# Attention scores split in two half-array parts in two planes, with single row maxima of one head beside score parts of another

## The reference, cut to what matters

```
q = src @ q_w ; k = src @ k_w ; v = src @ v_w        # 16 heads of 16
q = q scaled per head by a sigmoid-like gate of (q, scale_w), and by 16 ** -0.5
out = softmax(q @ k.T) @ v                           # per batch of 2048 tokens and head
```

## Time and profile before

| what | value |
|---|---|
| median of 3 runs | 2716.38 us (2714.47 to 2716.59) |
| the profiled execution | 2711.36 us |
| its span | 2709.6 us |
| mean granted clock of TensorE | 0.954 of full |
| busy PE / DVE / ACT / POOL | 93% / 80% / 64% / 32% of the span |

### The profile page before, as it was taken

The page is one execution under the profiler, slowest core; times in us unless marked ns, Lnnn a source line. Parts: engine busy times, 40 slices in busy tenths (PEclk is TensorE's granted clock), DMA queues, the critical chain, the costliest instruction groups (busy, mean ns, idle before and its releaser), DMA issues. The chain is left out here.

```text
span 2709.6 us, 40900 instructions
## 1 busy us (share of the span) xinstructions
PE 2507.0 (93%) x14248; PEld 1049.3 (39%) x14248; DVE 2172.1 (80%) x4357; ACT 1746.9 (64%) x2263; POOL 858.2 (32%) x991
## 2 busy tenths in 40 slices
PE   6799999999468999999999999999999999886995
PEld 6366666666341222222222222222222222464563
DVE  4577777787737889999899999898999995493885
ACT  2678877777130777777777777777777778322663
POOL 1377777777740111101110110111100000244563
PEclk9899999999785999999999999999999999886998
DMA  2322232222340030303004021030030000225884
GB/s 87 97 83 75 83 99 85 80 81 87 99 116 17 13 59 13 59 13 59 13 1 60 13 40 21 13 59 1 13 60 1 2 1 1 77 70 187 286 289 143
DMA packets 111524, 179.91 MB, mean 66 GB/s; under 512 B 18824, under 2 KB 85792, under 8 KB 106056
## 3 DMA queue, kind: packets, MB, share of 16 engines
q1 hardware_dynamic: 102984, 159.16, 22.0%
q0 software_dynamic: 6016, 15.41, 1.5%
q10 hardware_dynamic: 2320, 2.74, 0.3%
HBM read 150.42 MB, written 31.21 MB: 67 GB/s over the span
## 5 line engine op out<-in xcount | busy, mean ns | idle before, releaser
L1415 DVE TENSOR_REDUCE max_part<-round_psum 128x1 f32<-128x512 f32 x2048 | 1312.6, 685 | 107.3 <-PE round_psum L1344 93.5
L1387 ACT ACTIVATE p_exp<-score_psum 128x1024 f32<-128x1024 f32 x1024 | 992.5, 1022 | 282.7 <-PE score_psum L1332 282.5
L1364 PE MATMUL pv_psum<-p_exp,values 128*17 128x512 f32 x4096 | 539.7, 598 | 0.0
L1332 PE MATMUL score_psum<-q_stack,k_stack 99*128 99x512 bf16 (+1 forms) x2048 | 537.6, 383 | 1.5 <-DMA q_stack<-max_rows 0.7
L1344 PE MATMUL round_psum<-k_stack,q_stack 64*128 64x512 bf16 x2048 | 434.6, 395 | 15.4 <-DMA k_stack<-qk_rows 12.6
L1344 PEld LDWEIGHTS round_psum<-k_stack,q_stack 64*128 64x128 bf16 x2048 | 104.4, 93 | 687.0 <-DVE max_part L1415 565.2
L559 PE MATMUL rot<-tokens_t,w_in 128*128 128x512 f32 x576 | 274.5, 605 | 15.7 <-DVE bc_conv L697 12.7
L1332 PEld LDWEIGHTS score_psum<-q_stack,k_stack 99*128 99x128 bf16 (+1 forms) x2048 | 162.2, 98 | 259.4 <-ACT p_exp L1387 98.6
L1448 POOL CAST max_parts<-max_neg 128x16 bf16<-128x16 f32 x96 | 20.2, 211 | 655.3 <-DVE max_neg L1421 626.4
L766 POOL TENSOR_TENSOR decay<-cum_rows_in,scan_cum 128x1024 f32<-128x1024 f32 x64 | 121.4, 1897 | 109.0 <-PE y_psum L588 57.3
L941 POOL TENSOR_SCALAR q_scale<-q_scale 128x512 f32<-128x512 f32 x16 | 9.9, 618 | 434.3 <-ACT q_scale L923 434.3
(11 more groups left out here) (247 smaller groups left out, 3293.5 us busy)
## 6 DMA issues: line engine op xcount, KB each, us to landing
expert_w<-in_expert_w SPq DMA_DIRECT2D x39, 1028.0 KB, 5.7
cum_rows_in<-cum_rows SPq DMA_DIRECT2D x64, 512.0 KB, 3.8
cum_pairs_in<-cum_rows SPq DMA_DIRECT2D x120, 128.0 KB, 3.7
qk_rows<-qk_parts SPq DMA_DIRECT2D x64, 192.0 KB, 3.1
q_stack<-qk_rows SPq DMA_DIRECT2D x84, 128.0 KB, 7.7
k_stack<-qk_rows SPq DMA_DIRECT2D x84, 128.0 KB, 8.7
token_rows<-tokens SPq DMA_DIRECT2D x16, 512.0 KB, 3.4
x_in<-in_x SPq DMA_DIRECT2D x8, 512.0 KB, 8.5
```

The lines of the kernel that those rows point to most:

```text
L1332: m = nc.tensor.matmul(ebank[i][:, odd, :], ks[rows, n % 2, h, k * P:(k + 1) * P], qs[rows, n % 2, h, q * BLK:(q + 1) * BLK], start=True, ...
L1364: m = nc.tensor.matmul(pv[h * 32:h * 32 + VW, :], V[:, b * KT + k, g * HG + h, :], pt[:, (k * 2 + h // 2) % 4, h % 2, :], start=(k == 0), ...
L1387: nc.scalar.activation(pt[:, (k * 2 + i) % 4, :, :], ebank[i][:, :, :], ACT.Exp).then_inc(*exped.up(u, k, i))
L1415: nc.vector.tensor_reduce(mx[:, c * HG + h, keys:keys + 1], bank[step][:, :], AX_X, ALU.max).then_inc(*maxed.up(u, k, i))
```

## The change

Each head's rest rows (35) now lie in the same half of the array as its main rows, in a second plane of the stacks: head h has its main rows in plane `h // 2 * 2` and its rest rows in the plane after it. Heads 0 and 1 share these two planes, one in each half, as do heads 2 and 3. The number of rows moved by DMA into the stacks is the same; the zeros between are no longer needed.

A score is now two matmuls into the same bank that accumulate: `main` (64 rows, starts the sum) and `rest` (35 rows, ends it). In a step the twelve half-array matmuls stand in six pairs of neighbours, one in either half: maximum 0 and main 1; main 0 and rest 1; rest 0 and maximum 1; maximum 2 and main 3; main 2 and rest 3; rest 2 and maximum 3. Weighing and the due work follow. Main 1 and main 3 wait for ACT's reading of their tile a step ago; rest 0 and rest 2 release ACT; rest 1 of a unit's first step waits for the DMAs of the maximum rows.

```
-REST_AT = [slice(MAIN, MAIN + REST + MROWS), slice(0, REST + MROWS)]
+REST_AT = [slice(at.start, at.start + REST + MROWS) for at in MAIN_AT]
 MROWS_AT = [slice(at.stop - MROWS, at.stop) for at in REST_AT]
-ALL_AT = [slice(0, REST_AT[0].stop), slice(0, P)]
-GAP = slice(REST_AT[1].stop, MAIN)
+def main_of(h):
+    return MAIN_AT[h % 2], h // 2 * 2
+def rest_of(h):
+    return REST_AT[h % 2], h // 2 * 2 + 1
...
-            nc.sync.dma_start(dst[term_rows(t, odd), slot, odd::2, cols],
+            nc.sync.dma_start(dst[term_rows(t, odd), slot, t // 4::2, cols],
                               rows[odd]).then_inc(*S.stacked[slot].up(n, j, t, kind, odd))
...
                     for slot in range(2):
-                        for kind, tile, at, odd, rows in (("ones", S.ks, MROWS_AT[0], 0, gap[0:MROWS, :]),
-                                                          ("both", S.ks, slice(MROWS_AT[1].start, MAIN), 1, gap),
-                                                          ("gap", S.qs, GAP, 1, gap[MROWS:, :])):
-                            nc.sync.dma_start(tile[at, slot, odd::2, :].bitcast(F32),
-                                              over_mid(rows, HG // 2)).then_inc(*S.filled.up(slot, kind))
+                        for odd in range(2):
+                            nc.sync.dma_start(S.ks[MROWS_AT[odd], slot, 1::2, :].bitcast(F32),
+                                              over_mid(io["ones_rows"], HG // 2)).then_inc(*S.filled.up(slot, odd))
...
-        if scoring:
-            yield "score", u, k, 0
-            yield "score", u, k, 1
-        if ahead:
-            yield "max", mu, mk, 0
-            yield "max", mu, mk, 1
+        for left, right in ((("max", 0), ("main", 1)),
+                            (("main", 0), ("rest", 1)),
+                            (("rest", 0), ("max", 1)),
+                            (("max", 2), ("main", 3)),
+                            (("main", 2), ("rest", 3)),
+                            (("rest", 2), ("max", 3))):
+            for what, i in (left, right):
+                if what == "max" and ahead:
+                    yield what, mu, mk, i
+                if what != "max" and scoring:
+                    yield what, u, k, i
         if weighing:
             yield "weigh", *divmod(t - 1, KT), 0
-        if ahead:
-            yield "max", mu, mk, 2
-            yield "max", mu, mk, 3
         yield from due.get(t, [])
...
-                        nc.sync.dma_start(qs[MROWS_AT[h % 2], n % 2, h, q * BLK:(q + 1) * BLK],
+                        nc.sync.dma_start(qs[MROWS_AT[h % 2], n % 2, rest_of(h)[1], q * BLK:(q + 1) * BLK],
...
-                if what == "score":
+                if what == "main":
                     n, q = UNITS[u]
-                    if k == 0 and i == 0:
+                    rows, plane = main_of(i)
+                    if i % 2 and (u, k) != (0, 0):
+                        pe.wait_ge(*exped.at(*back(u, k, 1), i // 2))
+                    nc.tensor.matmul(ebank[i // 2][:, i % 2, :], ks[rows, n % 2, plane, k * P:(k + 1) * P],
+                                     qs[rows, n % 2, plane, q * BLK:(q + 1) * BLK], start=True, stop=False)
+                if what == "rest":
+                    n, q = UNITS[u]
+                    rows, plane = rest_of(i)
+                    if k == 0 and i == 1:
                         pe.wait_ge(*max_row[u % 2].at(u, HG - 1))
                         if u == 0:
                             pe.wait_ge(*S.filled.all())
-                    if (u, k) != (0, 0):
-                        pe.wait_ge(*exped.at(*back(u, k, 1), i))
-                    for odd in range(2):
-                        h, rows = i * 2 + odd, ALL_AT[odd]
-                        m = nc.tensor.matmul(ebank[i][:, odd, :], ks[rows, n % 2, h, k * P:(k + 1) * P],
-                                             qs[rows, n % 2, h, q * BLK:(q + 1) * BLK], start=True, stop=True)
-                    m.then_inc(*scored.up(u, k, i))
+                    m = nc.tensor.matmul(ebank[i // 2][:, i % 2, :], ks[rows, n % 2, plane, k * P:(k + 1) * P],
+                                         qs[rows, n % 2, plane, q * BLK:(q + 1) * BLK], start=False, stop=True)
+                    if i % 2 == 0:
+                        m.then_inc(*scored.up(u, k, i // 2))
```

More of the change, by code:

```diff
@@ L864, in __init__ @@
         self.loaded = sems.dma("w_qk_load", range(2))
-        self.filled = sems.dma("rows_fill", [(slot, what) for slot in range(2) for what in ("ones", "both", "gap")])
+        self.filled = sems.dma("rows_fill", [(slot, odd) for slot in range(2) for odd in range(2)])
         self.projected = sems.events("qk_projected", blocks)
@@ L1057, in _ @@
                 if (what, b) == ("load", NBLK - 1):
-                    gap = io["gap_rows"]
                     for slot in range(2):
-                        for kind, tile, at, odd, rows in (("ones", S.ks, MROWS_AT[0], 0, gap[0:MROWS, :]),
-                                                          ("both", S.ks, slice(MROWS_AT[1].start, MAIN), 1, gap),
-                                                          ("gap", S.qs, GAP, 1, gap[MROWS:, :])):
-                            nc.sync.dma_start(tile[at, slot, odd::2, :].bitcast(F32),
-                                              over_mid(rows, HG // 2)).then_inc(*S.filled.up(slot, kind))
+                        for odd in range(2):
+                            nc.sync.dma_start(S.ks[MROWS_AT[odd], slot, 1::2, :].bitcast(F32),
+                                              over_mid(io["ones_rows"], HG // 2)).then_inc(*S.filled.up(slot, odd))
                 if what == "residual":
@@ L1342, in _ @@
                         pe.wait_ge(*bank_read(before[step]))
-                    rows = MAIN_AT[h % 2]
-                    nc.tensor.matmul(bank[step][:, :], qs[rows, n % 2, h, at:at + P],
-                                     ks[rows, n % 2, h, keys * BLK:(keys + 1) * BLK], start=True,
+                    rows, plane = main_of(h)
+                    nc.tensor.matmul(bank[step][:, :], qs[rows, n % 2, plane, at:at + P],
+                                     ks[rows, n % 2, plane, keys * BLK:(keys + 1) * BLK], start=True,
                                      stop=True).then_inc(*summed.up(u, k, i))
@@ L1382, in _ @@
                 what, u, k, i = step
-                if what == "score":
-                    act.wait_ge(*scored.at(u, k, i))
+                if what == "rest" and i % 2 == 0:
+                    pair = i // 2
+                    act.wait_ge(*scored.at(u, k, pair))
                     if (u, k) >= (0, 2):
-                        act.wait_ge(*weighed.at(*back(u, k, 2), i))
-                    nc.scalar.activation(pt[:, (k * 2 + i) % 4, :, :], ebank[i][:, :, :],
-                                         ACT.Exp).then_inc(*exped.up(u, k, i))
+                        act.wait_ge(*weighed.at(*back(u, k, 2), pair))
+                    nc.scalar.activation(pt[:, (k * 2 + pair) % 4, :, :], ebank[pair][:, :, :],
+                                         ACT.Exp).then_inc(*exped.up(u, k, pair))
                 if what == "turn_rows":
@@ L2244, in layout @@
     o["v_w"] = kt(a["v_w"])
-    gap = np.zeros((MAIN - REST, SEQ // 2), np.uint32)
-    gap[0:MROWS] = 0x3F803F80
-    o["gap_rows"] = gap.view(np.float32)
+    o["ones_rows"] = np.full((MROWS, SEQ // 2), 0x3F803F80, np.uint32).view(np.float32)
     q = a["q_w"].reshape(KD, P, NG, HG * HD)
```

## The result

The changed kernel takes 2655.17 us (median of 4, 2651.04 to 2657.95), the kernel before 2716.49 (4 runs): a ratio of 0.9773, with a 95% interval of 0.9756 to 0.979. That is 61 us less; 52 were forecast. The profiled execution has a span of 2649.2 us, 60.4 less than before; 58.4 of that lie between the first and the last weighing of attention.

What follows compares the result with a forecast made beforehand. PE was taken to set the 2.60 us step, with DVE close behind. Terms -64 + 9 - 6 - 3 + 12 = -52 us gave 2716.4 - 52 = 2664; own range 2645 to 2690 (0.67), wider range 2630 to 2710.

Steps and rivals of the forecast that it cites:

- The step: A plain attention step falls from 2.60 to 2.47 us: -64 us over 492 steps with maxima.
- the first unknown: Whether a half's next load and matmul follow without a gap: 0 to 0.05 us per slot, taken as 0.
- (b): Weight loads show at the five slot boundaries: at 0.05 us each, a step of 2.65, kernel 2753; chance 0.09.
- (c): The full weight load shows, 0.10 us for each: a step of 2.90, kernel 2876; chance 0.02.
- The ring: Three banks rotate over four maxima per step; maximum 3 needs maximum 0's bank, so PE waits 0.07 us.
- Rival (a): Maximum 3's bank is already free by 1.10 us: a step of 2.40, -98 instead of -64, kernel 2630; chance 0.17.
- Rival (d): No change: DVE cannot start reduces closer than 0.65 us while PE writes the other banks; chance 0.05.
- Turned rows: Steps with turned rows keep the work and about 0.12 us of wait at maximum 2: 31 x 0.11 = -3 us.
- Negation: The negation delays maximum 3 by some 0.2 us, as now a maximum: nothing.
- Casts: In 28 steps with two casts ACT is late and main 3 stalls 0.3 us: +9 us.
- Turned output: DVE reduces maximum 0 only after the output's five operations: 1.08 us against 0.69 before, 31 x 0.39 = +12 us.
- Projections and scale matmuls: Now placed after weighing, they lose a bank wait: 0.14 x 42 = -6 us.

Runs made afterwards that it cites:

- the shortened reduce: Changed kernel with DVE's reduce of maximum 0 cut from 512 to 448 columns: 2626.65 us, ratio 0.9676.
- the run beside the moved output: The changed kernel itself, run on the same chip as a version with the turned output put between maximum 3 and weighing: 2652.16 us (that version 2648.55).

## Why the prediction was right, point by point

**The step.** 2.48 was seen where 2.47 was forecast. The slots follow each other 0.22 apart, so no load shows: the first unknown was taken right, and rivals (b) and (c) are out. Of the evidence for them, the three maxima of the earlier trace rows told the truth, and the 0.05 of the f32 scale matmul did not carry over. The ring costs what the chain of the earlier trace rows said: maximum 3 starts 1.18 after maximum 0 (forecast 1.17), and the shortened reduce shows that this link is the bound. Rival (a) is out. Rival (d) is too: DVE's reduces are 0.62 apart in a plain step, and 0.61 where DVE catches up behind a negation (its row further down). The other signs named are there as well: DVE is busy for all of the 7 us from 2200, neither main 1 nor main 3 waits in a plain step, and a step with turned output takes 3.56. One sign was too narrow: the load of maximum 2 waits for a bank too, at no cost. Between the medians, 2.604 and 2.474, lie 0.13 us a step, and 492 x 0.13 is 64 us, as forecast.

**The inserts** sum to about +5 us, where +12 was forecast. That is 7 of the 9 us by which the forecast fell short; the other 2 lie ahead of the first weighing. One of the five terms was right, the turned output. The other four, one of them put at nothing, were off by 4 to 9 us each, and partly cancel: that their sum came so near is luck. The prediction also missed what three of them share. It found that maximum 3 waits 0.07 us for its bank in every step, but not that another delay of PE in the same step runs inside this wait, and costs only what exceeds it. Rows of the changed kernel, first DVE around a negation, then PE at the weighings of the same stretch and at the turned rows:

```profile
2044.59 0.22 DVE L1435 TENSOR_REDUCE max_neg<-max_part 128x16 f32<-128x64 f32 x1
2044.92 4.96 DVE L1429 TENSOR_REDUCE max_part<-round_psum 128x1 f32<-128x512 f32 x8
```

```profile
2043.14 1.05 PE L1377 MATMUL pv_psum<-p_exp,values 128*17 128x512 f32 x8
...
2045.98 1.05 PE L1377 MATMUL pv_psum<-p_exp,values 128*17 128x512 f32 x8
...
2048.45 1.05 PE L1377 MATMUL pv_psum<-p_exp,values 128*17 128x512 f32 x8
2049.32 0.39 PE L1365 MATMUL round_psum<-const_ident_bf,max_parts 128*12 128x128 bf16 x4
2051.13 1.05 PE L1377 MATMUL pv_psum<-p_exp,values 128*17 128x512 f32 x8
```

- Turned rows: 2048.45 to 2051.13 is 2.68, so they cost 0.20 where 0.55 was paid before; 0.44 was forecast. The transposes start 0.87 after weighing, while a maximum starts 0.98 after it, and the wait of maximum 2 for its bank (0.07) runs inside that of maximum 3. That is -9 us instead of -3, for in four more cases, where a projection stands in the same step, nothing is gained.
- Negation: 2043.14 to 2045.98 is 2.84, a cost of 0.37. The prediction had some 0.2 for it before (the trace has 0.21) and put the difference at nothing. DVE has little slack (its eight reduces after it start (4.96 - 0.68)/7 = 0.61 apart), so the 0.33 from the negation to the reduce of the next maximum goes to the ring whole. Over the steps with a negation that is +4 us.
- Casts, forecast at +9. The timeline of PE and ACT in such a step:

```profile
1490.68 1.14 ACT L937 CAST qk_parts<-qk_raw 128x512 bf16<-128x512 f32 x2
1491.71 4.04 ACT L1401 ACTIVATE p_exp<-score_psum 128x1024 f32<-128x1024 f32 x4
```

```profile
1491.96 1.05 PE L1377 MATMUL pv_psum<-p_exp,values 128*17 128x512 f32 x8
...
1493.40 0.59 PE L1357 MATMUL round_psum<-k_stack,q_stack 64*128 64x512 bf16 x2
1493.71 0.49 PE L1335 MATMUL score_psum<-q_stack,k_stack 64*128 64x512 bf16 x2
...
1494.47 1.05 PE L1377 MATMUL pv_psum<-p_exp,values 128*17 128x512 f32 x8
```

ACT goes on to the exponentials 1.03 after it began the casts, not 1.2, for its operations overlap in the trace. Main 3 starts 0.31 after the line before, 0.09 late, where 0.3 was forecast; the ring had 0.07 of waiting to give, and the step takes 2.51 instead of 2.475. The place of the stall was right, but not its size or what it costs: some 0.03 us in about half of the 28 steps, under 1 us in all.

- Turned output, forecast 1.08, being its source:

```profile
2061.03 1.05 PE L1377 MATMUL pv_psum<-p_exp,values 128*17 128x512 f32 x8
2062.02 0.66 PE L1386 MATMUL round_psum<-const_f,pv_out 128*128 128x128 f32 x4
...
2062.71 0.26 DVE L1444 RECIPROCAL rden<-round_psum 128x16 f32<-128x16 f32 x1 [0.26 <-PE round_psum L1386]
...
2063.54 3.75 DVE L1429 TENSOR_REDUCE max_part<-round_psum 128x1 f32<-128x512 f32 x6
2063.68 0.39 PE L1357 MATMUL round_psum<-k_stack,q_stack 64*128 64x512 bf16 x1 [0.25 <-DVE tokens L1447]
...
2064.28 0.39 PE L1357 MATMUL round_psum<-k_stack,q_stack 64*128 64x512 bf16 x1
...
2064.59 1.05 PE L1377 MATMUL pv_psum<-p_exp,values 128*17 128x512 f32 x8
```

2061.03 to 2064.59 is 3.56: 1.08 to the hundredth. DVE starts 0.69 after the transposes, and maximum 3 comes 0.74 after the reduce of maximum 0, as worked out (0.69 and 0.75). Maximum 2 waits 0.25 us as well, for the bank of the transposes, which the prediction did not have; maximum 3 ends later, so it adds nothing.

- Projections and scale matmuls: -6 was forecast, about -2 came. PE's row of the changed kernel at a projection:

```profile
1461.21 1.05 PE L1377 MATMUL pv_psum<-p_exp,values 128*17 128x512 f32 x8
1462.19 1.98 PE L908 MATMUL round_psum<-tokens_t,w_qk 128*128 128x512 f32 x4
...
1464.11 0.39 PE L1357 MATMUL round_psum<-k_stack,q_stack 64*128 64x512 bf16 x1
...
1464.56 0.68 PE L1357 MATMUL round_psum<-k_stack,q_stack 64*128 64x512 bf16 x2
...
1465.61 0.62 PE L1377 MATMUL pv_psum<-p_exp,values 128*17 128x512 f32 x4
```

4.40 from weighing to weighing is 1.93 more than a plain step, against 1.96 before. The bank wait of 0.14 ahead of the projection is gone, as forecast. But the projection now holds PE for 1.92 (1462.19 to 1464.11), where it took 1.82: behind it come half-array matmuls instead of full-array scores, one more change of kind at 0.10, which the forecast left out. Maximum 2 also takes the projection's bank, which ACT must copy first (the pair of maxima takes 0.68, not 0.59); this too runs inside the wait of maximum 3, all but 0.02. A scale matmul takes 1.01 as before. Its step goes from 3.75 to 3.51, which is 0.11 of the 0.14 beyond what a plain step gains; there maximum 2 is 0.10 late.

The terms add up: -64 for the steps, 0, -2, -9, +4 and +12 for the inserts make -59, and -58.4 was measured from the first weighing to the last. The first weighing itself starts 2.2 us earlier, at 881.3 against 883.5. That can't be put down to the change: in the second trace of the same kernel (the run beside the moved output) it starts at 886.3. The prediction's books of the kernel before have a slip as well, 28 x 1.96 + 14 x 1.15 being 71 and not 69, so that 6 us were missing and not 8; no term of the forecast rests on it. The fewer filling DMAs bring nothing that the traces show: the first maximum starts at 821.18, against 821.30.

## What to carry to other kernels

Count the changes between kinds of matmul (full-array, half-array, narrow like the weighing), and not the matmuls alone: here each costs 0.10 us, and making scores and maxima the same half-array kind took two of four out of every step at the same number of streams. Once PE is faster, lay out the ring of banks again: here, with three banks and four users a step, the first user's matmul, its reduce and the release of its bank set the step; a shorter reduce there helped, and the same cut in another reduce did not. A wait that stands in every step also hides other delays of the step, up to its own length. Work moved to a new place should be checked against both its neighbours in the ring, the one whose bank it takes and the one that takes its own.

## What the runs showed of the hardware beyond that

The half-array stream is as tight as the full one. A 64-row main and the 35-row rest that accumulates into the same bank start 0.22 us apart in the same half, with the other half running beside them. Where the f32 scale matmul in two halves took 0.03 to 0.05 us more per pass than a full-array one, these bf16 matmuls take nothing more. The change of kind is paid between neighbours of different shape alone: the same four matmuls of a projection hold PE for 1.82 us ahead of full-array scores and for 1.92 ahead of half-array maxima. The bf16 transposes of the maximum rows start 0.87 us after weighing starts, 0.11 sooner than a maximum does, as if no change of kind were paid there. Both have weights of few columns (`128*17` and `128*12` in their rows), which may make them one kind; no run tests this.
